# VectorE's order in the attention steps: the maximum and the reciprocal of a step stand ahead of the context's and the new keys' low parts

## What is computed

```python
x = x + einsum('bct,bcd->bdt', x, weights[subjects])
q, k, v = x @ Wq.T, x @ Wk.T, x @ Wv.T            # per head, q and k normed and rotated
k_all = concatenate([k_cache[block_table], k], axis=1)
v_all = concatenate([v_cache[block_table], v], axis=1)
scores = einsum('bqhd,bkhd->bhqk', q, k_all) * SCALE   # masked where a cached key is not valid
probs = softmax(scores, axis=-1)
o = einsum('bhqk,bkhd->bqhd', probs, v_all)
x = x + einsum('bse,de->bsd', o, Wo)
```

## Time and profile before

| what | value |
|---|---|
| median of three runs | 1088.1 us |
| the profiled execution's own time | 1089.67 us |
| its span | 1087.9 us |
| TensorE busy | 1019.6 us (94%) |
| VectorE busy | 773.9 us (71%) |
| ScalarE busy | 709.5 us (65%) |
| GpSimd busy | 531.8 us (49%) |
| DMA, mean over the span | 257 GB/s |

### The profile page before, as it was taken

The page is one execution under the profiler, slowest core; times in us unless marked ns, Lnnn a source line. Parts: engine busy times, 40 slices in busy tenths (PEclk is TensorE's granted clock), DMA queues, the critical chain, the costliest instruction groups (busy, mean ns, idle before and its releaser), DMA issues.

```text
span 1087.9 us, 25187 instructions
## 1 busy us (share of the span) xinstructions
PE 1019.6 (94%) x8585; PEld 807.5 (74%) x8585; DVE 773.9 (71%) x1637; ACT 709.5 (65%) x1959; POOL 531.8 (49%) x650
## 2 busy tenths in 40 slices
PE   4899999999989777799999999999999999999998
PEld 2578888887768666668867877877876886886783
DVE  7779999999993776737846755854873873784681
ACT  4899999887752776736745744754763773674570
POOL 5455665568880355624633633552652652463340
PEclk9999999999999998999999999999999999999999
DMA  6789999999979489856974983973985895697440
GB/s 211 244 291 312 353 390 357 345 333 400 365 233 345 152 292 305 271 180 205 318 245 143 305 265 119 336 256 120 328 270 163 264 319 181 210 318 240 138 155 10
DMA packets 203888, 279.72 MB, mean 257 GB/s; under 512 B 26864, under 2 KB 158448, under 8 KB 202224
## 3 DMA queue, kind: packets, MB, share of 16 engines
q1 hardware_dynamic: 185072, 210.86, 58.4%
q0 software_dynamic: 18688, 67.25, 17.9%
HBM read 231.77 MB, written 46.27 MB: 256 GB/s over the span
## 4 chain that ended last, share of the span: by engine, by line
PE 58%; DVE 13%; issue 10%; ACT 8%; DMA 7%; POOL 2%; SPq 2%; DVEq 0%; ACTq 0%
PE ps_proj L1302 18%; PE ps_o L1302 15%; PE ps_o L1427 7%; PE ps_t L1402 5%; PE ps_s L1395 4%; DMA vs<-v_pages,v_row 4%; PE ps_s L1391 4%; DVE probs L1235 3%; ACT probs L925 2%; DMA wo_nat<-in_L_cond_Wo 2%; PE ps_rt L1357 2%; DVE c_stage L1158 2%; DVE rot L1130 1%; PE ps_o L1441 1%; POOL probs L797 1%
## 5 line engine op out<-in xcount | busy, mean ns | idle before, releaser
L797 POOL TENSOR_SCALAR probs<-probs,recip 128x544 f32<-128x544 f32 x256 | 187.0, 730 | 385.6 <-DVE recip L1243 383.5
L925 ACT ACTIVATE probs<-probs,neg_max 128x544 f32<-128x544 f32 x256 | 191.3, 747 | 160.3 <-DVE neg_max L1235 157.1
L1235 DVE CUSTOM_DVE_ANT_0 probs<-ps_s,mask,row_scale 128x544 f32<-128x544 f32 x256 | 199.9, 781 | 122.3 <-PE ps_s L1395 119.9
L1427 PE MATMUL ps_o<-pt_hi,vs 128*128 128x128 f16 x2048 | 214.8, 220 | 2.8 <-DMA vs<-v_pages,v_row 2.7
L932 ACT ACTIVATE pt_hi<-ps_t 128x512 f16<-128x512 f32 x256 | 149.2, 583 | 74.2 <-PE ps_t L1402 74.2
L1247 DVE SCALAR_TENSOR_TENSOR pt_lo<-ps_t,pt_hi 128x512 f16<-128x512 f32 x256 | 172.3, 673 | 21.5 <-ACT pt_hi L932 21.4
L1427 PE MATMUL ps_o<-pt_lo,vs 128*128 128x128 f16 x1024 | 186.1, 220 | 0.0
L751 POOL TENSOR_TENSOR roped<-rot 128x256 f32<-128x256 f32 x160 | 142.1, 910 | 83.3 <-DVE rot L1122 79.2
L1427 PEld LDWEIGHTS ps_o<-pt_hi,vs 128*128 128x128 f16 x2048 | 169.0, 98 | 8.9 <-DMA vs<-v_pages,v_row 4.2
L1302 PE MATMUL ps_proj<-wt_hi,x0t_hi 128*128 128x512 f32 x384 | 160.0, 417 | 7.7 <-DVE x0t_lo L1023 7.0
L1402 PE MATMUL ps_t<-fixed,probs 128*128 128x128 f32 x1024 | 156.6, 276 | 6.1 <-POOL probs L797 5.6
(11 more groups left out here) (147 smaller groups left out, 1721.8 us busy)
## 6 DMA issues: line engine op xcount, KB each, us to landing
kt<-k_pages_t SPq DMA_DIRECT2D x512, 128.0 KB
c_nat<-in_L_cond_k_cache SPq DMA_DIRECT2D x32, 512.0 KB, 6.1
q_t<-stage SPq DMA_DIRECT2D x64, 256.0 KB, 7.5
c_nat<-in_L_cond_v_cache SPq DMA_DIRECT2D x32, 512.0 KB, 6.8
qt<-q_t SPq DMA_DIRECT2D x32, 512.0 KB
w_nat<-in_L_cond_Wq SPq DMA_DIRECT2D x8, 1024.0 KB, 9.0
k_pages_t<-c_stage SPq DMA_DIRECT2D x16, 512.0 KB, 5.8
c_nat<-in_L_cond_Wo SPq DMA_DIRECT2D x16, 512.0 KB, 7.4
```

What stands on the lines that cost most here:

```text
L797: pool.tensor_scalar(probs_of(i), probs_of(i), col(recip, i), 1.0, ALU.mult, ALU.mult).then_inc(p_norm, 1)
L925: act.activation(pr, pr, ACT.Exp, bias=col(neg_max, i), scale=-1.0, accum_out=col(row_sum, i)).then_inc(a_exp, 1)
L1235: dve.tensor_tensor_reduce(out=probs_of(i), in0=ps_s[:, score_cols(i):score_cols(i) + KEYS], in1=mask[(i // HK) % 2][:, mask_at(i):mask_at ...
L1427: ins = pe.matmul(ps_o[n % 2][:, jl * P:(jl + 1) * P], v[:, part, :], p[i % NPT][:, c, :], start=jl == 0 and c == 0 and k == 0, stop=False ...
```

## The change

In VectorE's loop over the steps, the maximum and the reciprocal are issued before the low part of the new keys in all steps, and before the low part of the context in all steps but those with a projection.

```diff
             for i in range(STEPS):
                 if y_out(i) is not None:
                     add_residual(y_out(i))
-                if at(i, OE) is not None:
+                if at(i, OE) is not None and y_part(i) is not None:
                     ot_lo_of(at(i, OE))
-                if at(i, TNE) is not None:
-                    tn_lo(at(i, TNE))
                 if i + AHEAD < NP2:
                     masked_max(i + AHEAD)
                 if i + AHEAD - 1 < NP2:
                     row_recip(i + AHEAD - 1)
+                if at(i, OE) is not None and y_part(i) is None:
+                    ot_lo_of(at(i, OE))
+                if at(i, TNE) is not None:
+                    tn_lo(at(i, TNE))
                 if i < NP2:
                     t_lo(i)
```

## The result

The changed kernel takes 1071.0 us (median of four runs, 1069.3 to 1072.3) where the kernel before takes 1088.4; the ratio is 0.9842, 95% interval 0.9827 to 0.9858, so 17.4 us or 1.6% less. Run again in the first experiment, it took 1073.1 against 1087.6, ratio 0.9889, 0.9868 to 0.9911. The two intervals don't meet; the gain is somewhere between 10 and 19 us. Forecast were 13.3 us and 1074.8, in a range from 1067.0 to 1084.5.

What follows compares the result with a forecast made beforehand. TensorE was taken to bound the kernel from step 34 on, something else before. Gains of 12.3 us there and 4 us in steps 0 to 33, less 3 us to DMA, made 13.3 us: 1074.8 us, range 1067 to 1084.5.

Steps and rivals of the forecast that it cites:

- The bound: From step 34 on TensorE sets the pace, so only what stalls it counts, chiefly the second score pass waiting for `neg_max`.
- 12.3 us of stalls, less 3 given back to the DMA: Steps from 34 on: late-maximum stalls behind new-key and context steps go, 12.3 us; waits at sequence boundaries return 3 us.
- unknown room: Of 20 sequence boundaries outside the projections, six late today, the rest with unknown slack; so under half of 6.6 us.
- share 1.01: DMA engines' share through a 16.63 us sequence between projections, read as nearly full at 328 GB/s, about 1 us of slack.
- 40 x 0.22 and 10 x 0.35 as separate terms: From step 34 on: 40 waits behind new-key steps, 8.8 us, plus 10 behind late context steps, 3.5 us.
- Nothing for what stands behind the maximum: Low parts queued behind the maximum cost nothing, cover being at least a step, 1.8 us; without it 26 us over 63 steps.
- the sign that I had named: A wait of TensorE for `ptn` or `ot_lo` would show that the cover counted at nothing was not there.
- Steps 0 to 33, 4 us: First steps gain 4 us, between 0 and 18.8; kept low because each sequence is partly tied to the output weights' transfer.
- Rival 1: Waits for values or keys replace most of the removed stall; 4.5 us gained, 1083.6 us; chance 20%.
- Rival 2: A gather issued sooner delays the next sequence's keys, 1.4 us at each of 20 boundaries; slower, 1099.8 us; chance 4%.
- Rival 3: The change does nothing: the maximum would wait as long for its scores; 1088.1 us; chance 6%.
- The other page's rule: Skill page on DMA queues: engines alternate queues packet by packet, so a gather delays keys by up to what it moves.

Runs made afterwards that it cites:

- the first experiment: The changed kernel run once more, the same program, against the kernel before: 1073.1 us, 14.5 under before, ratio 0.9889.

## Why the prediction was right, and where it was off

- **The bound.** That TensorE's waits for `neg_max` are what counts behind step 34 was right: they went from 50 to 0, and the passes stand 0.33 to 0.34 us apart. The forecast place of the maximum (its scores plus at most 0.57 us) was met with 0.48 us behind the pass.
- **12.3 us of stalls, less 3 given back to the DMA.** In the profiles, the steps from 34 to 254 are 10.7 to 11.7 us shorter, where 9.3 stood, so the net was 1.4 to 2.4 us too pessimistic. By place in a sequence (the table above) both terms were near: the stalls were worth 13.4 us, and what the DMA took back was 3.2 and 3.9 us. The rest, 0.8 and 1.3 us, came from the projection steps, which the sum put at nothing because their matmuls cover the wait. The 3 us were worked out for late values, with "unknown room"; in the first profile all of the give-back is waits for keys, 3 in number, which the prediction named only as a possibility. That the size fits is therefore in part luck. Two readings under it were off: three of the six late gathers stand in steps 66, 130 and 194, the first projection steps, so 3 and not 6 of the 20 boundaries waited; and share 1.01 is one sequence, where three sequences between projections have 0.86 before and 0.91 and 0.93 in the changed kernel.
- **40 x 0.22 and 10 x 0.35 as separate terms.** As counts they hold: 40 waits stand behind new-key steps and 10 behind context steps. They are no prices of the two moves: moving the keys' part alone gives 9.5 us, moving the context's alone 4.2, and their sum, 13.7, is more than the 9.9 to 10.5 of both, because either move mends the context steps' waits.
- **Nothing for what stands behind the maximum.** Right from step 34 on: putting it back once more costs at most 0.9 us. In steps 0 to 33 the sign that I had named did appear: TensorE waits for the new keys' low part 3 times, 4.9 us. There ScalarE's high part of the new keys comes late behind its wait for an output weight, and VectorE has nothing to do but wait for it (2.6, 2.8 and 1.6 us), so it is this high part that holds TensorE up and not the maximum in front. ScalarE at one of the three:

```profile
394.15 0.72 ACT L953 ACTIVATE wo_hi<-wo_nat,scale 128x512 f16<-128x512 f32 x1 [3.20 <-DMA wo_nat<-in_L_cond_Wo]
394.77 0.36 ACT L939 ACTIVATE ptn<-ps_t 64x256 f16<-64x256 f32 x1
```

  I took the cover of "a step, 1.8 us" from the later steps. Here it is thinner: one place further back cost 2.5 to 3.0 us.
- **Steps 0 to 33, 4 us.** Measured 5.5 and 6.0. The size was low. Of the second pass's waits for `neg_max`, 18.8 us of idle weight loads there, 8.3 are left, less than half as forecast. The reason given for staying low, that each sequence is tied to a transfer, is not settled: the waits for the weights did grow, from 7.3 us to 12.7 and 12.1, as said, but moving their issue did not shorten the stage. Where the gain of this stage would end without the transfers stays open.
- **Rival 1** (the DMA takes most of it) fell, though its mechanism is there with 3.2 and 3.9 us. **Rival 2** (a gather gets ahead of the keys): waits for keys did appear, 3 in the first profile, 2.6 us, far from the 20 times 0.93 us from which on it decides. Whether a gather was in front of them, no run here tells. When the gathers were issued much earlier there were none, but those sequences were also 1.3 us longer, which gives keys and values more time. **Rival 3** fell with the 50 waits.
- **The Trainium skill**, "Perfetto Trace Analysis", Roofline, would have had nothing given back, with a ceiling of some 430 GB/s. By that the sum is 16.3 us. The traces do not agree: 3.2 and 3.9 us were given back, in the first profile at 302 and 304 GB/s over three sequences each, and less traffic made the changed kernel 5 us faster in its stretches. The other page's rule, engines taking turns between queues, no run here tells.

The forecast range held the result, and the medians of both comparisons lie within it. The 17.4 us of the first comparison are 4.1 more than forecast and the 14.5 of the second 1.2 more; by the stages behind step 0 the change is worth 17.2 and 16.7 us.

## What to carry to other kernels

In an in-order queue, put first what another engine waits for soonest, and ask of each thing moved back who reads it and in which step: the same operation was free to delay in 48 steps and cost nearly 0.8 us each in 14. Two stalls seen in one profile need not add up: one can hide the other (steps 50 and 51 here), and two moves can mend the same one. Summing step lengths by their place in the repeating pattern told more here than the list of waits: it kept what the change removed apart from what the DMA took. When a transfer is moved forward, look at the engine that issues it as well as at the DMA engines.

## What was not expected

- A gather's issue holds GpSimd for 0.93 to 1.03 us behind step 34, over all profiles. One between two products costs TensorE nothing here; two pairs with one product between them (5.5 us) made it wait 0.6 us on average, 40 times. A single pair wasn't tried.
- With less DMA traffic the kernel before waits more often for its maximum, 66 times instead of 50, and its stretches are 1.0 us longer, where those of the changed kernel are 5.1 to 5.6 us shorter. 14 of the 17 new waits behind context steps have no cause that a run here shows.
- The first 360 us, the same code, vary from execution to execution by 4 us (356.7 to 361.0); this is a quarter or more of the effect that was measured. It may be why two comparisons of the same pair gave 0.9842 and 0.9889; nothing here takes that apart.
